# Early stages, loads and order of a gated two-layer block kernel: base weights summed elsewhere, a shorter inverse root, a new order

## What is computed

```python
x = x + tanh(g_xattn[0]) * matmul(fake_quant(ln(x)), fake_quant(ctx))            # 8-bit levels, 512x512 per batch
x = x + tanh(g_ffn[0]) * (ln(x) @ W_base.T + b_base + low-rank update)           # update: masked coefficients, inverse real FFT
x = x + tanh(g_xattn[1]) * attention(ln(x), ctx, w_q, w_k, w_v, w_out, mask)     # 32 heads of 16, 8 key groups, 512 keys
x = x + tanh(g_ffn[1]) * bitlinear(relu2(bitlinear(ln(x), w_gate)) * bitlinear(ln(x), w_up), w_down)  # 1376 hidden, ternary weights
```

## Time and profile before

| | profiled execution |
|---|---|
| time / span | 267.79 us / 266.0 us |
| TensorE matmuls busy | 246.4 us (93%) |
| VectorE busy | 215.1 us (81%) |
| ScalarE busy | 185.3 us (70%) |
| GpSimd busy | 116.6 us (44%) |
| granted TensorE clock, mean | 0.986 of full speed |

### The profile page before, as it was taken

One profiled execution on the slowest core, in us unless ns is written; L12 is line 12 of the kernel. 1 busy time (PEld: TensorE's weight loads), 2 busy tenths in 40 slices (PEclk: granted clock), 3 DMA queues, 4 the chain that ended last, 5 costly groups with the idle time before them and its releaser, 6 DMA issues.

```text
span 266.0 us, 4711 instructions
## 1 busy us (share of the span) xinstructions
PE 246.4 (93%) x1482; PEld 120.8 (45%) x1482; DVE 215.1 (81%) x613; ACT 185.3 (70%) x311; POOL 116.6 (44%) x172
## 2 busy tenths in 40 slices
PE   8957697979999999999999999999999999996994
PEld 8622275834733334275334266424334244443442
DVE  2976974779898589796999976899788995889995
ACT  3710549969498998487687767998878988543541
POOL 7003312562233022464888754447989668100000
PEclk9999799999999999999999999999999999999899
DMA  6999985152855800000900380630000000000004
GB/s 174 390 369 415 383 365 124 25 122 27 302 186 132 156 10 0 4 0 26 155 0 0 92 346 2 131 48 0 4 2 0 2 0 1 2 0 0 0 2 158
DMA packets 8146, 27.63 MB, mean 104 GB/s; under 512 B 1402, under 2 KB 4010, under 8 KB 6490
## 3 DMA queue, kind: packets, MB, share of 16 engines
q1 hardware_dynamic: 7690, 21.63, 27.8%
q0 software_dynamic: 288, 5.70, 5.6%
q10 hardware_dynamic: 144, 0.00, 0.0%
HBM read 23.87 MB, written 3.41 MB: 103 GB/s over the span
## 4 chain that ended last, share of the span: by engine, by line
PE 60%; DVE 8%; ACT 4%; issue 3%; DVEq 0%; ACTq 0%
PE bank L776 11%; PE bank L803 10%; PE bank L754 10%; PE bank L779 6%; PE bank L826 5%; PE bank L696 4%; PE bank L844 4%; PE bank L762 3%; PE bank L686 2%; PE bank L811 1%; DVE fs L1280 1%; ACT ternary L955 1%; PE bank L863 1%; ACT big L985 1%; PE bank L677 1%
## 5 line engine op out<-in xcount | busy, mean ns | idle before, releaser
L1215 DVE CUSTOM_DVE_ANT_0 junk<-bank,maskb 128x512 bf16<-128x512 f32 x128 | 83.8, 686 | 13.2 <-PE bank L754 12.8
L985 ACT ACTIVATE big<-bank 128x512 f32<-128x512 f32 x128 | 74.6, 597 | 20.4 <-PE bank L776 14.5
L562 POOL TENSOR_TENSOR big<-big,product 128x512 int32<-128x512 int32 x48 | 61.1, 1274 | 37.4 <-ACT big L985 36.9
L776 PE MATMUL bank<-qst,kst 99*128 99x512 bf16 x128 | 48.9, 383 | 0.2
L754 PE MATMUL bank<-kst,qst 96*128 96x512 bf16 x128 | 48.0, 381 | 0.2 <-DVE mx L1215 0.2
L803 PE MATMUL bank<-big,vp 128*32 128x512 f32 x256 | 30.6, 598 | 0.0
L779 PE MATMUL bank<-ident_b,maskb 128*128 128x512 bf16 x80 | 30.4, 380 | 0.0
L572 POOL TENSOR_TENSOR mx<-mx 128x4 f32<-128x4 f32 x64 | 14.1, 220 | 20.8 <-DVE mx L1215 18.6
L754 PEld LDWEIGHTS bank<-kst,qst 96*128 96x128 bf16 x128 | 12.7, 99 | 22.4 <-issue 12.8
L776 PEld LDWEIGHTS bank<-qst,kst 99*128 99x128 bf16 x128 | 12.4, 97 | 20.7 <-ACT big L985 7.9
L606 POOL TENSOR_SCALAR stage_w<-stage_w,wscale 128x1376 f32<-128x1376 f32 (+1 forms) x12 | 17.7, 1476 | 7.5 <-DVE wscale L1337 7.5
(11 more groups left out here) (183 smaller groups left out, 411.3 us busy)
## 6 DMA issues: line engine op xcount, KB each, us to landing
stage_w<-in_w_down POOLq DMA_DIRECT2D x1, 2816.0 KB, 9.9
stage_w<-in_w_gate SPq DMA_DIRECT2D x1, 2752.0 KB, 21.7
stage_w<-in_w_up POOLq DMA_DIRECT2D x1, 2752.0 KB, 10.3
qst<-q_parts SPq DMA_DIRECT2D x18, 128.0 KB, 4.8
q_parts<-parts SPq DMA_DIRECT2D x12, 128.0 KB
x<-in_x SPq DMA_DIRECT2D x4, 256.0 KB, 12.3
big<-in_ctx SPq DMA_DIRECT2D x4, 256.0 KB, 5.1
big<-in_ctxT SPq DMA_DIRECT2D x4, 256.0 KB, 7.2
```

Of the source, the lines that this page charges most:

```text
L562: nc.gpsimd.tensor_tensor(p, p, keep[:, nt, KEEP_ST.index(i):KEEP_ST.index(i) + 1, :].broadcast_to([P, HG, P]), ALU.mult).then_inc(kept, 1)
L776: i = mm(o[:, :], kst[0:KM, b, g, s * P:(s + 1) * P], qst[0:KM, tile % 2, g * HG:(g + 1) * HG, :], start=True, stop=by_keep(c, s))
L985: fn(pt[:, c % 4, s, :], o[:, :], ACT.Exp).then_inc(drain(stage), 1)
L1215: v.tensor_tensor_reduce(junk[:, j % 2, :], o[:, :], maskb[:, tb(c // NG)[1], :], 1.0, HIDE, ALU.add, ALU.max, mx[:, c % 3, 0, hh:hh + 1]) ...
```

## The change

- **Base weights.** `we`: ScalarE copies each of the four pieces from PSUM into `we_sb`, a view of the buffer of the third ternary matrix; GpSimd adds it to `wT`. `y0` of tile 0 waits for the adds (`base_added`); `fabs` of matrix 2, which writes that buffer, waits for all four.
- **Column sums.** `csum` is scaled out of PSUM by ScalarE, not by VectorE.
- **Root.** Three Newton steps are replaced by another seed, a step of second degree (`w`) and one Newton step: for one column five instructions in place of six (one L1061 fewer), for three columns seven in place of nine.
- **Loads as stages.** Every load is a stage of the list with a place of its own. `wT` comes in four pieces with four semaphores, `dft` in two, `ctxT` of batch 1 in four.
- **Order.** `PREPARATION` and `FILL` are new. One filler stage of ten small matmuls is gone.

```diff
 PREPARATION = [
...
+    ("load_ctx", 3), ("warm", 0, 0, 42), ("load_ctx", 0), ("load_x", 0), ("scalars",), ("load_ctxT", 1),
+    ("warm", 0, 1, 60), ("products",), ("load_ctx", 1), ("xstats", 0), ("load_x", 3), ("load_ctx", 2),
+    ("load_adapters",), ("ln0", 0, 1), ("load_x", 1), ("load_x", 2), ("ln0", 0, 2), ("vones",), ("ln0", 0, 3),
+    ("ln0", 0, 4), ("cquant", 0), ("csum", 0), ("ln0", 0, 5), ("xstats", 1), ("ln0q", 0), ("load_dft", 0),
+    ("load_enc",), ("q1T", 0), ("warm", 0, 4, 10), ("xstats", 2), ("load_dft", 1), ("xstats", 3), ("load_wT", 1),
+    ("load_wT", 3), ("load_bias",), ("load_wT", 2), ("adapters",), ("ln0", 1, 1), ("ln0", 1, 2), ("load_wkv",),
+    ("ln0", 1, 3), ("ln0", 1, 4), ("ln0", 1, 5), ("ln0q", 1), ("r", 0), ("p", 0), ("vt",), ("pick",),
+    ("load_ctxT", 0), ("ln0r", 1), ("we",), ("load_mask",), ("ln1", 0, 0), ("load_ctxT", 3), ("k", 1, 0),
+    ("ln1", 0, 1), ("k", 1, 1), ("ln1", 0, 2), ("ln1", 0, 3), ("ln0", 2, 5), ("k", 0, 0), ("load_wT", 0),
+    ("load_ctxT", 6), ("load_ones",), ("q1T", 1), ("ln1", 0, 4), ("load_ctxT", 4), ("ln1", 0, 5), ("hT", 0, 1),
+    ("k", 0, 1), ("bias", 0), ("r", 1), ("load_ctxT", 5), ("load_gate",), ("y0", 0, 0), ("load_ctxT", 7),
+    ("ln0q", 2), ("y0", 0, 1), ("y0", 0, 2), ("ln0r", 2), ("mask",), ("k", 1, 2), ("load_ctx", 4), ("fabs", 0, 0),
+    ("y0", 0, 3), ("load_ctxT", 2), ("fabs", 0, 1), ("p", 1), ("y0up", 0), ("ln2", 0, 0), ("k", 0, 2),
+    ("fabs", 0, 2), ("ln2", 0, 1), ("load_wq",), ("ln2", 0, 2), ("v", 0, 0), ("fabs", 0, 3), ("ln2", 0, 3),
+    ("ln2", 0, 4), ("k", 0, 3), ("v", 0, 1), ("ln2", 0, 5), ("ksplit", 0), ("ln1", 1, 0), ("fsum", 0), ("v", 0, 2),
+    ("ln1", 1, 1), ("hT", 0, 2), ("cquant", 1), ("ln1", 1, 2), ("ln1", 1, 3), ("k", 1, 3), ("ln1", 1, 4),
+    ("v", 1, 0), ("ln1", 1, 5), ("v", 0, 3), ("q", 0, 0), ("fscale", 0), ("qsplit", 0), ("q", 0, 1), ("q", 0, 2),
+    ("q", 0, 3), ("ln0", 3, 5), ("v", 1, 1), ("bias", 1), ("hT", 1, 1), ("q1T", 2), ("fround", 0, 0), ("csum", 1),
+    ("y0", 1, 0), ("y0", 1, 1), ("y0", 1, 2), ("y0", 1, 3), ("ln0q", 3), ("v", 1, 2), ("ln0r", 3), ("y0up", 1),
+    ("vcopy", 0), ("qpick", 0, 0), ("r", 2), ("qpick", 0, 1), ("fround", 0, 1), ("fclamp", 0, 0), ("fclamp", 0, 1),
+    ("fround", 0, 2), ("fternary", 0, 0), ("p", 2), ("ln2", 1, 0), ("ln2", 1, 1), ("ln2", 1, 2), ("ln2", 1, 3),
+    ("q1T", 3), ("ln2", 1, 4), ("fclamp", 0, 2), ("fround", 0, 3), ("ln2", 1, 5), ("fclamp", 0, 3),
 ]
 FILL = {
...
+    1: [("v", 1, 3), ("hT", 1, 2)], 4: [("q", 1, 0)], 6: [("vcopy", 1)],
+    7: [("q", 1, 1), ("fternary", 0, 1), ("ksplit", 1), ("fternary", 0, 2), ("q", 1, 2)],
+    10: [("fternary", 0, 3), ("fload", 1), ("q", 1, 3)], 18: [("ln1", 2, 0)], 19: [("ln1", 2, 1)],
...
+    31: [("oT", 0), ("fsum", 1), ("y0", 2, 3)], 32: [("y0up", 2)], 34: [("fscale", 1)], 36: [("fround", 1, 0)],
+    37: [("fround", 1, 1)], 38: [("fclamp", 1, 0), ("keepT",)], 39: [("ln2", 2, 0), ("ln2", 2, 1)],
...
+    47: [("ln1", 3, 1), ("load_wo",), ("fternary", 1, 0)], 48: [("q", 2, 1), ("oT", 1)],
...
+    140: [("y1up", 2), ("ln3", 2, 0)], 143: [("gu", 1, 1, 1)], 145: [("aT", 3, 0)],
...
+    172: [("hidden", 1, 2)], 198: [("y1", 3, 0)], 207: [("aT", 3, 1)], 216: [("fq", 1, 0)], 218: [("y1", 3, 1)],
+    222: [("fq", 1, 1)], 229: [("fq", 1, 2)], 240: [("y1", 3, 2)], 271: [("y1", 3, 3)], 275: [("f1T", 2)],
+    284: [("f2T", 0, 0)], 304: [("y1up", 3)], 317: [("ln3", 3, 0)], 324: [("ln3", 3, 1)], 358: [("gu", 2, 0, 0)],
...
+                    for k in range(KT):
+                        pool.wait_ge(ld_wT[k], 16)
+                        wait_drained(pool, ("we", k))
+                        nc.gpsimd.tensor_tensor(wT[:, k, :], wT[:, k, :], we_sb[:, k, :], ALU.add).then_inc(base_added, 1)
...
+                    for k in range(KT):
+                        o = wait_filled(act, ("we", k))
+                        fn(we_sb[:, k, :], o[:, :], ACT.Copy).then_inc(drain(("we", k)), 1)
...
+                    fn(h2[:, :], o[:, :], ACT.Identity, scale=cst[:, NAZ1:NAZ1 + 1]).then_inc(drain(stage), 1)
...
+                    if k == 3:
+                        link(which, v.scalar_tensor_tensor(out=y, in0=w, scalar=5.0 * ROOT_G ** 2, in1=y, op0=ALU.add, op1=ALU.mult))
+                        after(which)
+                    if k == 4:
+                        link(which, v.scalar_tensor_tensor(out=y, in0=u, scalar=1.5, in1=y, op0=ALU.add, op1=ALU.mult))
...
+                    if k == 2:
+                        after(which)
+                        link(which, v.scalar_tensor_tensor(out=w, in0=u, scalar=-10.0 / 3.0 * ROOT_G, in1=u, op0=ALU.add, op1=ALU.mult))
```

More of the change, by code:

```diff
@@ L93 @@
 ]
 FILL = {
[3 rows of a table removed]
-    23: [("bias", 2)], 24: [("qsplit", 1)], 25: [("hT", 2, 1)],
-    26: [("y0", 2, 0), ("fabs", 1, 0), ("y0", 2, 1), ("fabs", 1, 1), ("fabs", 1, 2), ("y0", 2, 2), ("fabs", 1, 3)],
-    27: [("y0", 2, 3), ("y0up", 2)], 28: [("ln2", 2, 0)], 29: [("ln2", 2, 1), ("fsum", 1)],
-    30: [("ln2", 2, 2), ("p", 3)], 31: [("fscale", 1)], 33: [("fround", 1, 0), ("fclamp", 1, 0)], 34: [("keepT",)],
[5 rows of a table removed]
-    57: [("ln3", 0, 0)], 58: [("fclamp", 1, 2), ("bias", 3)], 59: [("fternary", 1, 1)],
[9 rows of a table removed]
-    91: [("fabs", 2, 3)], 93: [("fsum", 2)], 94: [("ln3", 1, 4), ("gu", 0, 0, 1)], 96: [("fscale", 2)],
@@ L119 @@
-    98: [("oT", 4)], 100: [("fround", 2, 0), ("hidden", 0, 0), ("gu", 0, 1, 0)], 102: [("gu", 0, 1, 1)],
-    103: [("fclamp", 2, 0)], 104: [("gu", 0, 2, 0), ("fround", 2, 1)], 106: [("ln3", 1, 5), ("fround", 2, 2)],
-    107: [("fclamp", 2, 1), ("hidden", 0, 1), ("fternary", 2, 0)], 108: [("ln3", 1, 6)], 109: [("fround", 2, 3)],
-    110: [("gu", 0, 2, 1)], 111: [("f1T", 1)], 114: [("aT", 2, 0)], 115: [("ffactors", 1), ("oT", 5)],
-    118: [("y1", 2, 0)], 119: [("aT", 2, 1), ("hidden", 0, 2)], 121: [("fclamp", 2, 2)], 122: [("fternary", 2, 1)],
@@ new lines @@
+    30: [("fabs", 1, 2), ("y0", 2, 0), ("y0", 2, 1), ("y0", 2, 2), ("fabs", 1, 3)],
+    31: [("oT", 0), ("fsum", 1), ("y0", 2, 3)], 32: [("y0up", 2)], 34: [("fscale", 1)], 36: [("fround", 1, 0)],
+    37: [("fround", 1, 1)], 38: [("fclamp", 1, 0), ("keepT",)], 39: [("ln2", 2, 0), ("ln2", 2, 1)],
[5 rows of a table added]
+    59: [("ln1", 3, 4), ("ln1", 3, 5)], 60: [("fternary", 1, 1)], 61: [("fclamp", 1, 2), ("bias", 3)],
[10 rows of a table added]
+    92: [("ln3", 1, 4)], 93: [("fsum", 2)], 94: [("gu", 0, 0, 1)], 95: [("fscale", 2), ("fround", 2, 0)],
@@ new lines @@
+    98: [("oT", 4)], 99: [("hidden", 0, 0)], 100: [("fclamp", 2, 0), ("gu", 0, 1, 0)], 102: [("gu", 0, 1, 1)],
+    104: [("ln3", 1, 5), ("ln3", 1, 6), ("gu", 0, 2, 0)], 105: [("fround", 2, 1)], 106: [("fternary", 2, 0)],
+    108: [("fround", 2, 2), ("hidden", 0, 1)], 109: [("ffactors", 1)], 110: [("gu", 0, 2, 1)],
+    112: [("fclamp", 2, 1)], 115: [("f1T", 1)], 118: [("aT", 2, 0)], 119: [("oT", 5)],
+    120: [("fclamp", 2, 2), ("hidden", 0, 2)], 121: [("fround", 2, 3)],
+    122: [("fternary", 2, 1), ("fternary", 2, 2), ("ffactors", 0), ("fclamp", 2, 3)], 123: [("fq", 0, 0)],
[22 rows of a table added]
@@ L342, in gated_blocks_kernel @@
         ld_x = [sem(f"x_loaded{t}") for t in range(NT)]
-        ld_scal, ld_dft, ld_coef, ld_wT, ld_wq, ld_wkv, ld_wo, ld_mask, ld_bias = (
-            sem(n + "_loaded") for n in ("scalars", "dft", "coefs", "wT", "wq", "wkv", "wo", "mask", "bias"))
+        ld_scal, ld_coef, ld_wq, ld_wkv, ld_wo, ld_mask, ld_bias = (
+            sem(n + "_loaded") for n in ("scalars", "coefs", "wq", "wkv", "wo", "mask", "bias"))
         ld_enc = sem("enc_loaded")
+        ld_dft = [sem(f"dft_loaded{i}") for i in range(KT // 2)]
+        ld_wT = [sem(f"wT_loaded{k}") for k in range(KT)]
         enc_cleared = sem("enc_cleared")
@@ L457, in _ @@
-            sp.dma_start(dft, dft_in).then_inc(ld_dft, 16)
-            sp.wait_ge(enc_cleared, 1)
-            for half in range(2):
-                sp.dma_start(enc[64 * half:64 * half + RR, :], enc_in).then_inc(ld_enc, 16)
-            sp.dma_start(wT[:, :, :], wT_in).then_inc(ld_wT, 16)
-            sp.dma_start(bias[:, :], bias_in.partition_broadcast(P)).then_inc(ld_bias, 16)
-            for t in range(1, NT):
-                sp.dma_start(x[:, t, :], x_in[:, t, :]).then_inc(ld_x[t], 16)
@@ L1047, in norm_part @@
                 stats, moments, newton = norm[which]
-                half, y, u = newton[:, 0, cols], newton[:, 1, cols], newton[:, 2, cols]
+                half, y, u, w = (newton[:, i, cols] for i in range(4))
                 if k == 0:
@@ L1065, in norm_part @@
                         link(which, v.tensor_tensor(u, u, half, ALU.mult))
-                    after(which)
-                    link(which, v.scalar_tensor_tensor(out=y, in0=u, scalar=1.5, in1=y, op0=ALU.add, op1=ALU.mult))
+                    if k == 2:
+                        after(which)
```

(1 more changed line is left out.)

108 lines of the change are left out of this document (62 added, 46 removed), and 82 rows, old and new, of tables (FILL, PREPARATION).

## The result

The changed kernel takes 261.22 us (median of four executions, 260.93 to 261.73), the kernel before 267.72 us beside it. The ratio is 0.9747, with a 95% interval of 0.9716 to 0.9778: 2.5% faster. The forecast was 262.7, in a range of 260.6 to 265.8. The profiled execution took 261.73 us with a span of 259.9, so the spans differ by 6.1 us (266.0 before). One execution further down, 269.39 us of the new preparation with the old steps, is of a slower state of the chip and is left out, which makes that kernel's median 266.26 and not 266.72.

A forecast was written before the change was run, and what follows sets the result against it. Bound: preparation hanging on w_gate's landing then 16.8 us of ScalarE, full TensorE in the steps, VectorE's work at the end. 267.79 - 4.1 (preparation) - 1.0 (end), steps 0, gives 262.7 us; range 260.6 to 265.8.

The forecast's parts named there:

- Landing of w_gate: Preparation: with 9740 KB instead of 12300 through, the w_gate load lands at 32.4 us, 6.1 us sooner.
- ctxT behind it: Preparation: third ctxT piece of batch 0, now behind w_gate, lands at 36.5 us; TensorE idles 2.3 us, costing 0.5.
- rival A: Preparation: TensorE's clock falls after the new idle stretch before 36.5 us, +1.2, time 263.9; chance with rival B together 0.18.
- Norm of tile 0: Preparation: the norm is ready at 25.7 us, and the 3.76 us that TensorE idled for it go.
- rival B: Preparation: GpSimd's four base weight adds hold VectorE's norm of tile 0, +2.0, time 264.7; chance with rival A together 0.18.
- Cover of the adds: Preparation: GpSimd's base weight adds have 3.4 us of cover, so cost zero; without it each late add costs 1.27.
- ScalarE's queue: Preparation: ScalarE is full from 39.1 us; `hT 1 1` is copied at 50.9, 4.5 us sooner, without a microsecond's gap.
- First scores: End of the preparation: first transposed scores at 67.7 us, not 71.84; term -4.1.
- Attention steps: Middle: TensorE's work is the same and only 1.3 us idle can be won; between -0.5 and +2, taken 0.
- Rival C: Attention steps: GpSimd's queue between score and maximum stalls TensorE; 264.6 or 271 us; chance 0.08 partly, 0.07 in full.
- The end: Three TensorE products no longer ahead of `y1 3 3`, -1.5; VectorE's added work behind it less the root, +0.5; term -1.0.
- rival D: Early gain larger: ctxT lands at 36.1 us and the steps' idle 1.3 us go too; 260.9 us; chance 0.10.

The follow-up runs named there:

- the reverse mix: Changed kernel's code with loads and stages in the old order up to the first transposed scores, in the new order behind them; 267.50 us.

## Why the prediction was right, step by step

- *Landing of w_gate*: forecast 32.4, measured 32.28. Counting the KB ahead of a load in the queue and dividing by the rate of two landings was good to 0.1 us. Such a 0.1 is partly luck: with the load late in the changed kernel 38.5 was expected and 37.9 came, with the load early in the old one about 31 and 29.4. The experiments that move the load alone confirm the mechanism.
- *ctxT behind it*: forecast 36.5, measured 36.19. The new idle stretch of TensorE was 0.77 and not 2.3 us, since TensorE came there late. Nothing was lost for rival A: the granted clock didn't fall behind it. It fell elsewhere, over 15 to 20 us, behind an idle 4.57 us that the walk had passed over.
- *Norm of tile 0*: forecast 25.7, measured 27.7. The step that failed is "Zero" for the base weights' effect on VectorE; rival B had the mechanism right and its size too large: it put 4.4 to 5.1 us on the norm's path, of which 1.3 to 2.0 would reach the end. Measured are 2.0 on the norm; `hT 0 1` ran at 28.6, 1.0 late, and the run with the adds on VectorE, whose norm is later still, ends no later. The rule quoted there from the Trainium skill (SBUF — State Buffer, Who interferes with whom) agrees: the one-column instruction with two inputs took 1.26 us beside the adds and 0.15 without. The same section says that VectorE's tensor_scalar, which has one tensor input, can run in a mode that takes the shared port pair too, and that is what I left out: "few of the instructions there have two inputs" is true, but those with one stood as well, 1.45 and 1.49 for 0.55 and 0.48. The adds themselves were over at 30.2, not at 28.6: GpSimd began them at 24.75, 1.2 later than forecast.
- *Cover of the adds*: I said 3.4 us and 1.27 for each late add. Twice the adds (5.5 us more) cost nothing. Part of that is cover: `y0 0` takes its four sums one at a time, with key products between, and the wait for ctxT lies behind it. But at the key split ScalarE was still 1.0 us late (40.10 for 39.10), and 0.7 came back only because VectorE's subtraction came out ahead of GpSimd. Without that `hT 1 1` would have been some 0.5 late (an estimate from these rows: 50.73 + 0.73 for 50.98), still less than the 2.1 that a cover of 3.4 gives.
- *ScalarE's queue*: forecast `hT 1 1` copied at 50.9, measured 51.56. The difference is one instruction of VectorE, the subtraction (L1225) of the query split, 1.46 us instead of 0.69. It lies beside GpSimd's scale of the ternary weights, which started first, and it ends 0.54 after that one ends (48.46 + 1.41 = 49.87). The other traces bear that out: started 0.22, 0.38, 0.49 and 0.85 us behind that scale it takes 1.73, 1.56, 1.46 and 1.11, and always ends 0.54 after it; with GpSimd silent it takes 0.69, and in the two runs on the adds, where VectorE starts first, 0.73. The wait of 1.60 us that this gives ScalarE is over the microsecond that I had named as the longest gap in that queue:

```profile
48.95 1.46 DVE L1225 TENSOR_TENSOR qs<-qs,parts 128x512 f32<-128x512 f32 x1 [1.55 <-ACT parts L978]
```

```profile
48.46 1.41 POOL L634 TENSOR_SCALAR stage_w<-stage_w,wscale 128x1376 f32<-128x1376 f32 x1
```

- *First scores*: forecast 67.7 (-4.1), measured 68.23 (-3.6). The term is 0.5 too large. The instruction just named (0.8) would account for it, but the first scores of the four profiles with this same start lie 0.4 apart, so 0.5 is hardly more than scatter.
- *Attention steps*: forecast 0, measured -0.9 to -1.1. This is the term that was mis-sized. With the new preparation and the old steps (the `woT` load behind the query parts) `y1 3 3` ends at 234.11, with the new steps to the last one at 232.99; 0.2 of these 1.1 lie already between their first exponentials (69.06, 68.82). "1.3 us idle is all there is to win" bounded it well; I took 0 where 0.9 to 1.1 was won. The gain belongs to the steps, whatever the preparation: from the first to the last exponential it is 154.6 to 154.8 us in the three kernels with the old steps and no long wait, 153.0 in eight with the new ones, 153.3 in the changed kernel's own profile and 153.6 with the root of before. Some 0.7 of that difference comes back behind the last exponential, where more other work is left. TensorE's timeline with the old steps has waits of 0.17, 0.20 and 0.41 us (the last for ScalarE's copy ahead of a gate product) that the new steps don't have, 0.8 in all; the rest is too finely spread to be named. Rival C's queue on GpSimd did not form: no wait of TensorE between 69 and 231 us reaches 0.2 us. A queue did cost 2.2 us, on SyncE, but only in the mix of new preparation and old steps, where `load_wo` has a place that neither kernel gives it. For the move of `load_wo` in the change itself "zero" is not contradicted: with that load issued at 21.56 (the reverse mix) the new steps take their 153.0 as well.
- *The end*: forecast -1.5 for `y1 3 3` and +0.5 behind it; measured -1.56, and +0.56 for what moved there less 0.44 to 0.52 for the root (forecast 0.3), so +0.1.
- *The sum*: -3.6 - 1.1 - 1.56 + 0.1 = -6.2, against 6.1 between the spans. Forecast was -5.1. The forecast was 1.5 us too high by the medians, and of this the steps are 1.1 and the tail 0.4, against 0.5 the other way in the preparation; the remaining 0.4 is the scatter between the profiled pair and the medians. So the errors partly cancel. 261.2 lies just below the band that got 0.52, in rival D's, which got 0.10. D had two parts: ctxT did land at 36.2, but the first score was not early for it; the idle time won in the steps is the part that came.
